# Eight final waits on the landing of the tile writes move from SyncE's program to the end of GpSimd's

## The reference

```
x = x + graph_layer(layernorm(x), adj)          # K = 3 hops: X W0 + T X W1 + T T X W2, relu
                                                # T = rows of adj * exp(leaky_relu(..)), made to sum to 1
h = layernorm(x)
route, prob = argmax and max of softmax(h @ switch_w.T + switch_b)   # 16 experts
pos = how many earlier tokens chose the same expert
y = h @ expert_w[route].T + expert_b[route]     if pos < capacity (1.2 * tokens / 16), else h
out = x + y * prob
```

## Time and profile before

| what | value |
|---|---|
| median of 3 runs | 742.04 us (741.46 to 742.31) |
| the profiled execution's own time | 743.05 us |
| its span | 741.3 us |
| outside the span in it | 1.75 us |
| TensorE busy in the span | 707.4 us (95%) |
| VectorE, ScalarE, GpSimd busy | 639.5, 480.8, 456.6 us |
| tile writes, line 587 | 143, mean 1018 ns |

### The profile page before, as it was taken

One profiled execution on the slowest core, in us unless ns is written; L12 is line 12 of the kernel. 1 busy time (PEld: TensorE's weight loads), 2 busy tenths in 40 slices (PEclk: granted clock), 3 DMA queues, 4 the chain that ended last, 5 costly groups with the idle time before them and its releaser, 6 DMA issues.

```text
span 741.3 us, 17931 instructions
## 1 busy us (share of the span) xinstructions
PE 707.4 (95%) x4714; PEld 620.0 (84%) x4714; DVE 639.5 (86%) x3129; ACT 480.8 (65%) x1509; POOL 456.6 (62%) x542
## 2 busy tenths in 40 slices
PE   8999999999999999999999999999999999968784
PEld 7888788788998998888989989889888888857673
DVE  6899999999998999999999989999999998867462
ACT  3567677667666667676676766676767667654451
POOL 6446666546666676666666666766666666565554
PEclk9999999999999999999999999999999999987997
DMA  9976565534443454444354334444443322254430
GB/s 283 206 181 159 158 167 155 145 117 149 130 131 124 155 158 152 151 151 148 127 156 139 120 122 154 155 140 152 143 131 135 109 102 90 86 175 144 117 108 6
DMA packets 95458, 104.33 MB, mean 141 GB/s; under 512 B 10729, under 2 KB 85622, under 8 KB 95360
## 3 DMA queue, kind: packets, MB, share of 16 engines
q1 hardware_dynamic: 77104, 65.97, 30.1%
q0 software_dynamic: 15376, 34.30, 14.7%
q10 hardware_dynamic: 2880, 2.92, 1.6%
HBM read 54.13 MB, written 54.76 MB: 147 GB/s over the span
## 4 chain that ended last, share of the span: by engine, by line
PE 86%; DVE 6%; issue 3%; ACT 1%; DMA 1%; POOL 1%; another core or an unknown queue 0%; SPq 0%; POOLq 0%; DVEq 0%; ACTq 0%
PE ps_z12a L1359 11%; PE ps_z12b L1359 11%; PE ps_lgb L1359 9%; PE ps_z0a L1359 8%; PE ps_z0b L1359 7%; PE ps_lga L1474 6%; PE ps_z0a L1442 4%; PE ps_z0b L1442 4%; PE ps_z12b L1421 4%; PE ps_xt L1461 4%; PE ps_xt L1389 3%; PE ps_lgb L1505 3%; PE ps_z12a L1421 3%; PE ps_t L1435 2%; PE ps_t L1410 2%
## 5 line engine op out<-in xcount | busy, mean ns | idle before, releaser
L587 POOL DMA_INDIRECT out<-lent,tok x143 | 145.6, 1018 | 156.2 <-DVE lent L1273 134.7
L574 POOL DMA_INDIRECT rowbuf<-rows,idx x128 | 130.3, 1018 | 52.4 <-issue 27.4
L652 ACT CAST xth<-ps_xt 128x256 fp32r<-128x256 f32 x128 | 47.9, 374 | 95.7 <-PE ps_xt L1389 94.8
L519 POOL TENSOR_SCALAR x<-xin,nm,r 128x256 f32<-128x256 f32 x128 | 84.5, 662 | 16.5 <-PE ps_xt L1389 10.5
L726 ACT ACTIVATE x<-rin 128x255 f32<-128x255 f32 x143 | 86.8, 608 | 3.1 <-DMA rin<-rowbuf 2.4
L1474 PEld LDWEIGHTS ps_lga<-swc,xft 128*128 128x128 f32 x512 | 76.5, 190 | 10.8
L707 ACT ACTIVATE od<-rows,oc,oa 128x256 f32<-128x256 f32 x128 | 77.0, 602 | 0.1
L1474 PE MATMUL ps_lga<-swc,xft 128*128 128x16 f32 x512 | 65.7, 242 | 0.0
L948 DVE TENSOR_TENSOR em<-e 128x128 f32<-128x128 f32 x128 | 40.1, 314 | 26.1 <-ACT e L674 25.1
L868 DVE TENSOR_TENSOR xtl<-ps_xt,xth 128x256 fp32r<-128x256 f32 x128 | 53.9, 421 | 9.4 <-ACT xft L699 7.6
L673 ACT ACTIVATE e<-ps_t,svs 128x128 f32<-128x128 f32 x128 | 47.1, 368 | 22.7 <-PE ps_t L1435 20.6
(11 more groups left out here) (223 smaller groups left out, 2363.1 us busy)
## 6 DMA issues: line engine op xcount, KB each, us to landing
rin<-rowbuf SPq DMA_DIRECT2D x143, 130.0 KB
out<-od SPq DMA_DIRECT2D x32, 512.0 KB
xin<-in_x SPq DMA_DIRECT2D x31, 512.0 KB, 4.4
ain<-in_adj SPq DMA_DIRECT2D x32, 256.0 KB, 4.6
ewr<-in_ewT SPq DMA_DIRECT2D x16, 256.0 KB, 3.9
ewr<-negs POOLq DMA_DIRECT2D x16, 256.0 KB, 5.1
out<-lent,tok POOLq DMA_INDIRECT x143
rowbuf<-rin ACTq DMA_DIRECT2D x1, 2080.0 KB, 20.1
```

The lines of the kernel that those rows point to most:

```text
L519: pool.tensor_scalar(x0[:, g % 2, :], xin[:, g % BODY, :], nm1[:, q, g % G:g % G + 1], r1[:, q, g % G:g % G + 1], ALU.add, ALU.mult).then_ ...
L574: pool.indirect_dma_start(out=rowbuf, out_offset=bass.IndirectOffsetOnAxis(ap=idx[:, i:i + 1], axis=0), in_=rows[:, r, :], in_offset=None, ...
L587: pool.indirect_dma_start(out=out.rearrange("g n d -> (g n) d"), out_offset=bass.IndirectOffsetOnAxis(ap=tok[:, i % RY:i % RY + 1], axis=0 ...
```

## The change

The loop of eight waits leaves the end of SP's program and stands, with the same semaphores and the same counts, behind the last `scatter(i)` of GpSimd's. Nothing else is changed: SP's last instructions are now its two waits for `d_out`.

```diff
@@ -469,8 +469,6 @@
                 load_tiles(i, min(G, NT - i))
             for par in range(2):
                 sp.wait_ge(d_out[par], 16 * (B // G // 2))
-            for r in range(RY):
-                sp.wait_ge(b_sc[r], 16 * len(range(r, NT, RY)))
 
 
         @block.gpsimd
@@ -629,6 +627,8 @@
                 row_scatter(IT, g)
             for i in range(WOVEN + 1, NT):
                 scatter(i)
+            for r in range(RY):
+                pool.wait_ge(b_sc[r], 16 * len(range(r, NT, RY)))
 
 
         @block.scalar
```

## The result

| | before | changed |
|---|---|---|
| median | 742.14 us (740.64 to 742.82, 22 runs) | 743.38 us (741.52 to 745.63, 22 runs) |
| ratio of the runs | | 1.0021, 95% interval 1.0014 to 1.0028 |
| profiled execution: time, span | 743.05, 741.3 us | 742.19, 740.5 us |

What follows compares the result with a forecast made beforehand. GpSimd's closing DRAIN was taken to set the end: starting at 736.9 and lasting 5.0 us, it ends at 741.9 instead of 741.08, +0.8 us on the median 742.04, giving 742.8 us, range 737.8 to 744.0.

Steps and rivals of the forecast that it cites:

- The end is set by GpSimd's DRAIN, not by SP's waits: Program's end: GpSimd's DRAIN runs to 741.08 us and releases the barrier, which SP reaches 4.1 us too early.
- SP's part gives 0: End of SP's program: without the eight waits SP arrives some 15 us earlier, but had 4.1 us to spare, gaining 0.
- The delay of the start, 1.4 us: GpSimd's closing DRAIN would start at 736.9 us behind the moved waits, 1.4 us after its last write leaves at 735.53.
- W: Length of GpSimd's closing DRAIN when it starts with everything landed; taken as 5.0 us, half way between 4.4 and 5.55.
- +0.8 us: Net forecast at the program's end: GpSimd's DRAIN ends at 741.9 instead of 741.08 us.
- Same: Whole kernel's time changes by no more than 0.2%, 1.5 us; chance 0.51, with the case of no effect included.
- slower: Whole kernel slows by more than 0.2%, from a closing DRAIN of 5.7 us on; chance 0.22.
- the likeliest case: Closing DRAIN of 4.4 to 5.7 us behind the waits: +0.2 to +1.5 us, 742.2 to 743.6 us; chance 0.45.
- The rival of the slow wait: GpSimd's long DRAIN slowly checks writes in flight, so it is short once all landed: 738.0 us, or 740.6; chance 0.27.
- the whole length is its own work: GpSimd's DRAIN overlaps nothing with the landing: 5.55 + 0.27 = 5.82 us, end +1.6 us, 743.7 us; chance 0.22.
- The rival that the 5.55 us run on from the last write: Closing DRAIN's time counts from the last write whoever waits, so the end stays: 742.0 to 742.2 us; chance 0.06.
- The bound from below, 0.17 us: Lower bound for the closing DRAIN's length, from POOL's DRAIN at program start, where no DMA had been issued.

Runs made afterwards that it cites:

- the single write: Program of GpSimd alone, no computation: one indirect write of 128 rows not waited for, then a DRAIN; the write lands at 22.6, the DRAIN ends at 22.7 us.
- the late DRAIN: Changed kernel with a GpSimd memset of 128 x 3840 float32 and a wait for it ahead of the DRAIN; 727.84 us against 722.87 of the kernel before.
- the group of 32: Program of GpSimd alone, no computation: 32 indirect writes of 128 rows, each landed, then a DRAIN, which took 2.66 us.
- the sweep: GpSimd alone, computation left out: groups of 16 to 128 landed indirect writes, a DRAIN behind each; 9.18 us at 112, 1.51 at 124, 1.83 at 128.

## Why the prediction was right, and where it was off

- **"The end is set by GpSimd's DRAIN, not by SP's waits."** Right. Taking the DRAIN away gives 0.59%, 4.3 us (3.3 to 5.2), against the 4.1 us between SP's arrival and the DRAIN's end.
- **SP's part gives 0.** Right: both waiting is 1.0015 (1.0006 to 1.0024), which can't be told from the change.
- **The delay of the start, 1.4 us.** 734.7 - 733.20 = 1.5 us was measured. The missing 0.1 us come from the step that took 736.9 instead of SP's 737.0, for three semaphore records that GpSimd would be spared. But behind the landing SP has only two wait records, both starting at 736.7, and GpSimd has two as well, both at 734.4; from there to the DRAIN it is 0.3 us on either.
- **W, the DRAIN's length with everything landed, "half way between 4.4 and 5.55".** This is the term that was mis-sized: 5.0 was taken, 5.54 measured, the upper of the two. The error is in the reason given for splitting the 1.2 us between the last write's record and its landing. I asked whether these were waiting or work; they were both at once. The DRAIN does wait for landings (the single write shows it), but it had 67 DMAs to clear at 0.081 us each, and had enough to do with the landed ones until long after the last landing. So nothing of its length was waiting that the moved waits could have taken over. The run that waits for all but the last write shows this: started with that write in flight, the DRAIN takes 5.542 us too. Hence +1.50 + 5.54 - 5.55 = +1.5 us in place of +0.8; the measured 1.6 us is twice the forecast.
- **"Same", within 0.2%, was given 0.51 and "slower" 0.22.** The ratio of 1.0021 lies on that bound, with an interval on both sides of it, so which of the two came true can't be said. The length (5.54) is in the likeliest case's own range, 4.4 to 5.7; the time, 743.4 us, is also in its range of 742.2 to 743.6. The time alone would prove little: the range of 737.8 to 744.0 took in cases of both signs. It is the DRAIN's record that bears the mechanism out.
- **The rival of the slow wait** (a short DRAIN behind the waits) fell: with everything landed the DRAIN took 5.54 us. The rule of the Trainium skill weighed with it ("PSUM — Partial Sum Buffer", section "Engine vs sequencer instructions") says that a drain waits for the engine to go fully idle. The trace agrees as far as that goes: behind a single write the engine's record ended at 21.16 us and the DRAIN at 22.7. But it ended only with the landing, 22.6, and the rule tells neither of that nor of the 0.081 us for each DMA, which is what counts here.
- **The rival "the whole length is its own work"** had the right mechanism with one part too many: 0.27 us for a start behind a wait, which the DRAIN's record doesn't show. Its sum of +1.6 us is the measured one, in part by luck: 0.27 too much in the DRAIN, 0.1 too little in its start.
- **The rival that the 5.55 us run on from the last write** fell with the late DRAIN: 3.3 us more of waiting, the same 5.542 us.
- The bound from below, 0.17 us at the program's start, was a row of the right instruction under the wrong condition: no DMA had gone before. The prediction names that, and it was the key: length goes by the DMAs since the last DRAIN.

## What to carry to other kernels

Look at which engine's DRAIN ends last before you move a closing wait. A wait ahead of a long DRAIN adds its whole exposed time, 1.5 us here; the same wait on an engine that is early costs nothing. Where GpSimd issues DMAs, its closing DRAIN here costs 0.081 us for each that it hasn't cleared, and if every DMA is already waited for by a semaphore, leaving that DRAIN out of the block gave more (4 to 5 us) than the placing of the waits (1.5 us).

## What the runs showed of the hardware that was not expected

- A DRAIN of GpSimd takes 0.034 us with nothing since the last one and 0.081 us for each DMA since, whether landed just now or up to 100 us earlier, as the first writes of the group of 32: 0.13, 0.71, 2.66, 5.92 and 9.18 us for 1, 8, 32, 72 and 112 writes.
- Between 112 and 124 writes the engine clears 106 of them by itself, as read from the slope; a DRAIN behind 124 takes 1.51 us. No gap among the writes shows when. So one more or one fewer DMA could change a kernel's closing DRAIN by up to some 8 us; that is an estimate from the sweep, and wasn't tried in this kernel, where steps of 106 don't give the 67 that are left.
- A DRAIN in the middle of a program holds GpSimd until its earlier work is done and its DMAs have landed. Its record, 4.2 us in the median, is more than it costs: under the graph layer the kernel lost 0 to 4 us by 32 of them together, and in the last phase the engine stood still 2.1 to 5.2 us at each.
- The changed kernel's 22 runs spread over 4.1 us, those of the kernel before over 2.2 us. With both engines waiting the spread was 1.1 us, so the place of the waits is not shown to be the cause; it stays open.
